# Eight of the 32 key tiles of each attention unit summed from half-precision parts: one core, a layer of tanh-gated attention and a quantized feed-forward

## What is computed

```python
x_norm = layernorm(x, gamma, beta)
q, k = l2_normalize(x_norm @ w_q), l2_normalize(x_norm @ w_k)      # per head
v = x @ w_v
align = einsum('bhqd,bhkd->bhqk', q, k)
resonance = 0.5 + 0.5 * tanh((align - 0.27) * 15)                   # = sigmoid(30 * (align - 0.27))
gate_q, gate_k = (0.25 + 0.75 * sigmoid(dot(z, g)) for z, g in ((q, g_q), (k, g_k)))
fused = einsum('bhqk,bhkd->bhqd', resonance * gate_q * gate_k, v)   # no softmax, no normalization
x1 = layernorm(x + fused @ w_o + b_o)
h = silu(fp4(x1) @ fp4(w_gate).T) * (fp4(x1) @ fp4(w_up).T)         # 704 wide
out = layernorm(x1 + fp4(h) @ fp4(w_down).T)
```

## Time and profile before

| | before |
|---|---|
| median of 3 runs | 4404.63 us (4399.64 to 4407.42) |
| the profiled execution | 4404.2 us, its span 4402.4 us |
| PE busy | 4119.8 us (94%) |
| ACT busy | 4021.6 us (91%) |
| DVE busy | 1562.0 us (35%) |
| POOL busy | 159.4 us (4%) |
| granted TensorE clock, mean | 0.993 |

### The profile page before, as it was taken

How to read it: one execution, slowest core, us unless ns; L and a number is a source line. 1 busy time by engine, 2 the same in 40 slices (tenths; PEclk the granted TensorE clock), 3 DMA queues, 4 the chain that set the end, 5 groups by cost and what they waited for, 6 DMA issues and landing times.

```text
span 4402.4 us, 80654 instructions
## 1 busy us (share of the span) xinstructions
PE 4119.8 (94%) x28776; PEld 1290.5 (29%) x28776; DVE 1562.0 (35%) x4540; ACT 4021.6 (91%) x3271; POOL 159.4 (4%) x120
## 2 busy tenths in 40 slices
PE   7988899999999999999999999999999999999997
PEld 5651222222222222222222222222222222222223
DVE  6754023323332333333233323333333333333236
ACT  4669999999999999999999999999999999999993
POOL 2330000000000000000000000000000000000001
PEclk9999999999999999999999999999999999999998
DMA  3454443344434433444344434443344334433440
GB/s 109 127 127 78 70 76 58 60 77 77 61 60 73 78 62 62 70 78 65 62 68 77 71 56 68 77 71 61 63 77 72 60 62 77 77 58 60 77 82 13
DMA packets 179953, 314.46 MB, mean 71 GB/s; under 512 B 65264, under 2 KB 141808, under 8 KB 154608
## 3 DMA queue, kind: packets, MB, share of 16 engines
q1 hardware_dynamic: 179568, 309.41, 41.5%
HBM read 266.82 MB, written 42.47 MB: 70 GB/s over the span
## 4 chain that ended last, share of the span: by engine, by line
PE 68%; ACT 16%; issue 8%; DVE 4%; DMA 2%; SPq 2%; POOL 0%; ACTq 0%; POOLq 0%; DVEq 0%
PE ps L1269 34%; PE ps L1259 19%; ACT room L698 15%; PE ps L1296 8%; PE ps L1319 4%; DMA m_f<-fused_t 2%; DVE room L850 1%; SPq L523 1%; SPq L499 1%; PE ps L1214 0%; PE ps L1281 0%; DVE st L804 0%; DVE xnT L840 0%; PE ps L1225 0%; PE ps L1206 0%
## 5 line engine op out<-in xcount | busy, mean ns | idle before, releaser
L698 ACT ACTIVATE room<-ps 128x1024 f32<-128x1024 f32 (+1 forms) x2816 | 3790.7, 1415 | 183.1 <-PE ps L1259 167.3
L1269 PE MATMUL ps<-room,vt 128*32 128x512 f32 x16384 | 2052.8, 602 | 0.0
L1259 PE MATMUL ps<-qs,room 64*128 64x512 f16 x8198 | 1325.9, 383 | 213.8 <-ACT room L698 192.6
L1259 PEld LDWEIGHTS ps<-qs,room 64*128 64x128 f16 x8198 | 310.8, 93 | 1758.3 <-ACT room L698 1107.0
L1269 PEld LDWEIGHTS ps<-room,vt 128*32 128x32 f32 x16384 | 388.4, 108 | 947.0 <-issue 947.0
L1296 PE MATMUL ps<-wguT,m_xqT 128*128 128x352 f32 x960 | 348.2, 485 | 0.0
L959 DVE TENSOR_TENSOR vz<-ps,vz 128x352 f32<-128x352 f32 x120 | 63.0, 525 | 757.7 <-ACT vz L708 757.7
L964 DVE TENSOR_TENSOR vz<-ps,vz 128x352 f32<-128x352 f32 x120 | 63.0, 525 | 595.8 <-PE ps L1296 595.8
L1319 PE MATMUL ps<-wdnT,wqk 128*128 128x256 f32 x720 | 198.9, 404 | 0.6 <-DVE wqk L929 0.6
L1296 PEld LDWEIGHTS ps<-wguT,m_xqT 128*128 128x128 f32 x960 | 162.6, 189 | 105.1 <-issue 54.3
L592 POOL TENSOR_TENSOR m_x<-m_x,bo 128x256 f32<-128x256 f32 x60 | 43.8, 730 | 3890.9 <-DMA m_x<-in_L_attn_x_dram 3890.9
(11 more groups left out here) (172 smaller groups left out, 2206.4 us busy)
## 6 DMA issues: line engine op xcount, KB each, us to landing
room<-k_parts SPq DMA_DIRECT2D x520, 256.0 KB, 9.2
vt<-v_gated SPq DMA_DIRECT2D x65, 1024.0 KB, 17.5
...
gqb<-q_gates SPq DMA_DIRECT2D x256, 64.0 KB, 2.1
...
fused_t<-fs SPq DMA_DIRECT2D x256, 32.0 KB, 1.6
...
```

Source lines behind the costliest of these rows:

```text
L698: act.activation(res[:, c, o:o + m, :], ps[:, o:o + m, :], ACT.Sigmoid, scale=2 * SHARP / QK_UP ** 2, bias=-2 * SHARP * THRESH).then_inc(b ...
L1259: ins = pe.matmul(ps[:, BANK[n % 2] + i, :], ks[o:o + HROWS, par, h // 2, kt * P:(kt + 1) * P], qs[o:o + HROWS, par, h // 2, :], start=Tru ...
L1269: ins = pe.matmul(ps[32 * h:32 * h + 32, SUM_BANK, :], vt[:, par, n * HD:n * HD + 32], r, start=kt == 0, stop=kt == KT - 1, skip_group_che ...
```

## The change

- Of the key tiles `3c` those with `c` in `SPLIT = [0, 1, 2, 4, 5, 6, 7, 8]` (8 of 32 in each unit, from `j = 1` on) are no longer summed in float32. Their four results are one group of four banks. VectorE makes `r_hi` = half precision of 4096 times the result, and `r_lo` = the rest, in half precision (`split_results`, two instructions over 128 x 2048). GpSimd makes the parts of the values. TensorE then does for each head two half-precision matmuls (`split_sums`): one with `r_hi`, one with `r_lo` as the moving operand, both against 32 weights, 16 of the high and 16 of the low part of the values; so there are two sums for each head, in two sets of 16 rows.
- The sums of such a tile stand four groups later: behind group `4c + 4` instead of `4c`.
- Key tile 1 is summed first, with 32 weights of which 16 are zero (`vp`), and the other tiles by 16 weights instead of 32.
- The two rows of sums are stored apart: eight DMAs at the end of a unit instead of four, and two loads, `m_f` and `m_f2`, which GpSimd adds before piece P (`l_fs`). There is also one small load more for each unit (`vp`).
- GpSimd scales all values of a unit by a power of two (`scale_values`), for which stage A finds the largest value: two VectorE instructions more for each block in `inverse_roots`, and a short exchange between VectorE and TensorE at its end.
- In the tail the projection takes four matmuls instead of two, and the loads of x stand behind the last stores.

```diff
-        at[4 * c + 2] = [0, 1] if c == 0 else [3 * c + 1]
+        at[4 * c + 2] = [1, 0] if c == 0 else [3 * c + 1]
+def split_at(n):
+    return [SPLIT.index(c) for c in SPLIT if 4 * c + 4 == n]
+SPLIT = [0, 1, 2, 4, 5, 6, 7, 8]
+def is_split(kt):
+    return kt % 3 == 0 and kt // 3 in SPLIT
...
+                ins = pool.tensor_scalar(vt[:, par], vt[:, par], v_up, None, ALU.mult)
+                ins = pool.tensor_scalar(vp[:, par], vp[:, par], v_up, None, ALU.mult)
...
+                for v, hi, lo in parts:
+                    ins = pool.tensor_scalar(v, v, 1 / RES_UP, None, ALU.mult)
+                for v, hi, lo in parts:
+                    ins = pool.tensor_copy(hi, v)
+                for v, hi, lo in parts:
+                    ins = pool.tensor_tensor(lo, v, hi, ALU.subtract)
...
                     pool.tensor_tensor(m_x[:, :], m_x[:, :], bo[:, :], ALU.add).then_inc(l_xb, 1)
-
+                    pool.wait_ge(l_f, 32 * (k + 1))
+                    pool.tensor_tensor(m_f[:, :, :], m_f[:, :, :], m_f2, ALU.add).then_inc(l_fs, 1)
...
+                    after(dve.tensor_reduce(vmx[:, TB:2 * TB], vz[:, par, :, 0:D], AX_X, ALU.max,
+                                            apply_absolute_value=True))
+                    after(dve.tensor_tensor(vmx[:, 0:TB], vmx[:, 0:TB], vmx[:, TB:2 * TB], ALU.max))
...
+            def split_results(u, g, i):
+                n = 4 * SPLIT[i]
+                r = res[:, (NGRP // 2 * g + n // 2) % RES_CYCS, 0:HG, :].rearrange("p h n -> p (h n)")
+                if i >= 2:
+                    dve.wait_ge(b_pv, u * KT + SPLIT_POS[i - 2] + 1)
+                dve.wait_ge(b_act, u * NGRP + n + 1)
+                after(dve.tensor_scalar(r_hi[i % 2], r, RES_UP, None, ALU.mult))
+                dve.scalar_tensor_tensor(out=r_lo[i % 2], in0=r, scalar=RES_UP, in1=r_hi[i % 2],
+                                         op0=ALU.mult, op1=ALU.subtract).then_inc(b_cv, 1)
...
+                    split_results(u, g, 2)
+                    begin_quantize(k, par)
+                    if ends(j, g):
+                        end_tile(k - 1, 1 - par)
+                    split_results(u, g, 3)
+                    turned(k)
+                    split_results(u, g, 4)
+                    for p in range(4):
+                        gates(k, (p,))
+                        if p < 3:
+                            split_results(u, g, 5 + p)
+                    hidden(k)
...
+            def split_sums(i, par):
+                for part in (r_hi[i % 2], r_lo[i % 2]):
+                    for h in range(HG):
+                        ins = pe.matmul(ps[32 * h:32 * h + 32, SUM_BANK, :], vh[:, par, i, 32 * h:32 * h + 32],
+                                        part[:, h * BLK:(h + 1) * BLK], start=False, stop=False, skip_group_check=True)
...
-                    pe.wait_ge(l_f, 16 * (k + 1))
+                    pe.wait_ge(l_fs, k + 1)
...
-                        sums(kt, par, g)
+                            pe.wait_ge(b_v, u + 1)
+                        if not (split and is_split(kt)):
+                            sums(kt, par, g)
+                    for i in split_at(n):
+                        if split:
+                            pe.wait_ge(b_cv, (u - HG) * NSPLIT + i + 1)
+                            split_sums(i, par)
```

183 lines of the change are left out of this document (146 added, 37 removed).

## The result

| | before | changed |
|---|---|---|
| median | 4402.14 us (4399.57 to 4407.42, 4 runs) | **4784.97 us** (4749.54 to 4802.53, 4 runs) |
| ratio | | 1.0859 (95% interval 1.0811 to 1.0906) |
| the profiled execution, its span | 4404.2, 4402.4 us | 4749.54, 4747.7 us |
| granted TensorE clock, mean | 0.993 | 0.973 |

The kernel is 8.6% slower: the direction is as predicted (4576 us, 4505 to 4690), the size is 209 us off and outside the range.

The account below looks back on a forecast made before the run. The prediction took ScalarE's own pace plus about 4.6 us of gaps a unit as the bound. Units at -0.7 + 2.3 + 0.7 = +2.3 us, times 60, gave 4404.2 + 138 + 21 + 7 + 6 = 4576 us, range 4505 to 4690.

Parts of the forecast that it names:

- What bounds: Unit loop: ScalarE's own steps take 57.9 of 62.5 us; only its gaps, about 4.6 us a unit, can be won.
- Split sums on TensorE, -0.7: Key tiles on TensorE: a split tile costs 0.43 instead of 0.86 us; gaps won less longer cycles, -0.7 us a unit.
- The split of group 16, +0.7: VectorE's split of group 16 ends late, TensorE waits 0.9 us and ScalarE loses 0.7: +0.7 us a unit.
- The way to P, +2.3: More stores, a second load and GpSimd's addition make TensorE wait 2.3 us at piece P; ScalarE loses it all.
- GpSimd, "nothing, if it does not disturb VectorE": GpSimd's pass over the values and seven small instructions, 6 to 10 us a unit, cost nothing if VectorE is undisturbed.
- a rival with 20% and +98 us: VectorE's splits and GpSimd's scaling hold each other up, split of group 24 late: +1.6 us a unit, 4674 us; 20%.
- VectorE's instruction: First instruction of each split on VectorE, a tensor_scalar over 2048 elements, takes 1.23 us at two elements per cycle.
- the rival at one element per cycle: First split instruction runs at half that rate, 2.28 us: +1.5 us a unit at the split of group 16, 4666; 10%.
- Once, +34: Costs outside the repeated units: stage A +21 us, start of unit 0 +7, tail +6.

Follow-up runs that it names:

- e13: Changed kernel with constant scale, query gates' loads last, one run of eight splits (c = 1 to 8), sums stored by head, normalization later: 4387.5 us.
- e4: Changed kernel with values scaled by a constant (no GpSimd pass) and the query gates' loads issued behind those for piece P: 4479.8 us.
- e9: Changed kernel with constant scale, gates' loads last, six split tiles, four two-plane stores, and normalization behind the split of group 16: 4588.4 us.
- e12: e4 with sums kept in DRAM by head, four one-plane stores, four loads, and GpSimd adding the sums before the bias: 4453.6 us.
- e1: Changed kernel with values scaled by a constant, without the search for the largest value or GpSimd's pass over the values: 4621.2 us.
- e3: Kernel before with only the changed way to piece P (doubled stores, two loads, GpSimd's addition), no splits and no scaling: 4574.0 us.
- e15: Changed kernel with GpSimd's scaling of the next unit's values begun only after VectorE has made all eight splits: 4696.3 us.
- e10: Changed kernel with 10 half-precision matmuls that nobody reads put ahead of piece P's wait in each unit: 4693.6 us.

## Why the prediction was right and wrong

**What bounds: right.** ScalarE's own steps sum to 57.7 us a unit (57.9 worked out) and hold in every kernel wherever a group shows no gap, and only the gaps moved the time of a unit. In e13 TensorE has 149 us less work, and 9 us come of it.

**Split sums on TensorE, -0.7: the price right, the balance nearly.** From the starts in e4 a split tile takes 0.55 us from its first matmul to the next scores and a float32 tile 0.99: 0.44 less, where 0.43 was predicted. The gaps at 5, 7, 11, 19, 27, 31 and 35 went. Those at 14, 15, 38 and 39, the cycles behind groups 12 and 36, went from 1.17 us together to 2.71 in e4: 1.5 more, as worked out. All gaps of e4 but that at group 10 sum to 4.77 against 4.72 before: with the late split of group 16 (next point) the balance is 0, as forecast.

**The split of group 16, +0.7: right.** The gap at group 23 is 0.99 against 0.33, and it goes when the normalization is moved (e9, e13). It does not come of P being late: it is 1.00 in e4 and e12 as well.

**The way to P, +2.3: this is one of the two steps that failed.** It cost 3.55. The wait itself was sized well: 2.7 us of TensorE's (2.3 predicted), P at 11.74 - 0.25 = 11.5 after the first store (11.0). The term that is missing from the sum is what the wait does to the clock, put at nothing without a word. TensorE idles 2.7 us on average, the granted clock falls to 1.2 GHz behind P in 35 of 59 units, and P and the next scores run at half speed with ScalarE waiting. In the 22 units without any low stretch the gaps at 10 and 11 sum to 2.44, in the 30 with one to 4.70; but late units are also those that lose the clock. Units with equal waits give the price without that: in the changed kernel, e1, e3 and e15, where TensorE idled 2.0 to 2.5 us before P, the two gaps sum to 2.51 in 37 units without a low stretch there and to 4.13 in 26 with one (mean waits 2.24 and 2.23). So a low stretch costs 1.6 us; times 35 of 59 units that is 1.0 of the 3.55, an estimate, and the wait has the other 2.5. e10 shows it by an edit: 23 of the 35 stretches gone, 86 us won. The Trainium skill (TensorE: Matmul & The Clock Gate, HAM oscillation — how this bites in real kernels) describes just this, a wait in every round that puts TensorE back to the lower clock each time. The trace agrees in kind, though here it is not each time: 35 of 59 units. The profile of before already held a hint of the sort, since its only low stretch in the loop lies in a unit whose gaps sum to 6.4 instead of 4.8.

**GpSimd, "nothing, if it does not disturb VectorE": the second that failed.** It cost 1.5 us a unit. I had this as a rival with 20% and +98 us; e15 gives 84 and e1 1.5 us a unit. The mechanism was the one described, but it already reaches the split of group 20, whose gap (1.01 at group 27) is the larger one; the rival had only that of group 24 and the next. GpSimd's work was also undersized: the pass and its seven small instructions take 12.1 us undisturbed (e15) and 17.6 here, where 6 to 10 were predicted. What the forecast did wrong was to take one of the two cases as the term, at zero, although the timeline had both engines at work from +35 to +41. The rule of the Trainium skill (SBUF — State Buffer, Who interferes with whom) holds in these traces in both directions, with one exception. VectorE's tensor_scalar, begun inside GpSimd's pass, lasted up to 6.4 us instead of 1.22 and ended 1.08 us after the pass, so it waited for nearly all of it; GpSimd's pass, begun beside VectorE's two-source instruction, lasted up to 7.6 instead of 5.44, and its addition 2.1 on average instead of 0.73 (e4). The exception is the two-source instruction begun inside the pass: in all 21 cases it ended 0.4 us after it, although it takes 2.29 alone, so it did not wait in full.

**VectorE's instruction: right.** 1.218 us alone; the rival at one element per cycle falls.

**Once, +34: too small by 8.** The first sigmoid starts 28.3 us later (21 predicted), unit 0 is 10.3 longer (7), the end 3.3 (6). The 7 us too little are not in the exchange at the end: VectorE's reduction over the squares (L928) is already 27.6 us late in the last block. The new reduction took 1.21 us, as worked out, but a block grew by 1.6 to 1.7 instead of 1.4, and five blocks by 2.3 to 3.3. In each of these five the changed kernel's trace has a stretch at the lower clock (132.1, 152.6, 190.1, 231.1 and 268.6 us), and before there was none there. So the clock cost some 6 us here too, an estimate from these differences.

Together, a unit grew by 5.1 us: 3.55 behind P (2.3 predicted), 1.5 behind the meetings of VectorE and GpSimd (0), and 0.1 of all else (0). The profiled execution is 35 us below the median of its own runs, whose clocks are 0.966 to 0.968 against its 0.973; so this kernel's times, which scatter by 53 us where the kernel before has 8, go with the clock. The range should have held the sum of forecast and rival with the clock's cost. It stopped at each rival alone.

**What stays open.** Why e13 wins 0.3 us a unit and no more is shown group by group (gaps of 0.69, 0.56, 0.84 and 0.46 at 10, 14, 39 and 38, where before had 0.13, 0.25, 0.42 and 0.08), but no version here is free of all of them; by these rows, bringing those at 10, 38 and 39 back to what they were before would win 1.4 us a unit more, an estimate that no run shows. Why a wait of the same length loses the clock in some units and not in others was not found.
